# GpSimd's extra piece of an attention step directly behind the masking of the keys, ahead of its wait for the statistics

## The chip, the cores and the metric

The kernel runs on one core of one Trainium2 chip. TensorE (PE) multiplies matrices, VectorE (DVE), ScalarE (ACT) and GpSimd (POOL) work element by element, SyncE (SP) issues DMAs. The metric is the device time of one execution in microseconds. The kernel before takes 1256.31 us (median of 3 runs, 1255.82 to 1256.45).

## What is computed

Two layers on `x` of 128 sequences x 64 positions x 128 features, float32. Cut to what matters:

```python
x = x + xattn0(layernorm(x), ctx, ctx)     # 16 heads of 8, causal softmax attention
x = x + ffn0(layernorm(x))                 # 64 experts, the top 8 by affinity, sigmoid weights
x = x + xattn1(layernorm(x), ctx, ctx)     # autocorrelation attention (rfft, top 6 lags)
x = x + ffn1(x)                            # ternary weights, clipped activations

def xattn0(q, k, v):
    qh, kh, vh = split(q @ Wq + bq), split(k @ Wq + bq), split(v @ Wq + bq)
    scores = einsum('bhqd,bhkd->bhqk', qh, kh) / sqrt(8) * mask - 1e10 * (1 - mask)
    return merge(einsum('bhqk,bhkd->bhqd', softmax(scores), vh)) @ Wo + bo
```

The change lies in the first of these four, the function `attention`. While it runs, other engines' spare time also goes to preparing the second: the experts' weights are split into a high and a low part (the low part is the weight less its rounded high part), and the first chunk's norm and routing (which experts a token takes, with which weights) are computed in its last steps.

## The kernel before

`attention` works on 64 tiles, two sequences of 64 positions on the 128 partitions. It is a pipeline written by hand: each engine has one `step(t, r)`, called for t = 0 to 69, in which it does one stage of several tiles at once, each by its lag behind t. Steps 0 to 15 are written out, steps 16 to 47 are a loop of four steps (r = t mod 4, 8 turns), steps 48 on are written out again. Inside an engine the order is the order of the code; between engines only semaphores order the work.

In a step t the stages that matter here are:

- GpSimd: `expand` of tile t-3 (L405, "masking": the keys are spread over four heads with a mask of heads), which waits for ScalarE's copy of the queries and keys (L543); then, for tile t, variance plus epsilon (L428), which waits for VectorE's aggregate, and the power -1/2 (L430); then the bias added to the residual of tile t-5 (L433); then, in some steps, an extra piece.
- VectorE: reciprocal (L289) and scaling (L294) of tile t-6, which wait for TensorE's weighing; the shift of the scores of tile t-4 (L283); the norm of tile t-1 (L273, one `tensor_scalar` from SBUF to SBUF); the statistics of tile t (L264, L268); the output added to the residual of tile t-6 (L300), which waits for TensorE's output projection (L652); in some steps a piece of routing; the row maximum of tile t-3 (L278), which waits for TensorE's scores.
- TensorE: weighing of the values of tile t-6 (L647), which waits until VectorE's L300 of the tile before has freed the bank; transposes (L608, L615, L626, L630), projections (L637, L638, L652); mask and scores of tile t-3 (L594, L600), which wait for GpSimd's masked keys.
- ScalarE: the high part of the weights (L568, one piece in each looped step), copies out of PSUM, the exponential (L558).

The extra pieces of GpSimd are: in steps 13 and 14 two pieces of the chunk norm (L738, L745); in the loop the low part of the weights (L413), of the up weights in steps with r = 1 and of the down weights in steps with r = 3, 16 in all; in steps 48 to 51 and 57 to 60 the split of the biases (L465 to L496); in steps 52 to 56 the routing's ends (L858 to L861), its two powers (L866), the denominator (L870) and the routing's low part (L841). The norm's roots in step 12 and the routing's weights (step 61) and gates (step 63) are further ones. The code of the low part waits for the high part:

```python
def low_part(t, k):
    cols = bass.ds((t // 4 - peeled // 4) * piece, piece)
    wait_apart(pool, high, t + 2 * k + 2, idle["pool"])
    nc.gpsimd.tensor_tensor(cst[("wul", "wdl")[k]][:, cols], raw[:, k, cols], ...)
```

Of the kernel before, what the change touches and what calls it, by code (L numbers as in the profile page):

```python
# [27 lines left out]
ALU = mybir.AluOpType  # L28
# [20 lines left out]
def at_least(eng, sem, value):  # L49

    if isinstance(value, int) and value <= 0:
        return
    eng.wait_ge(sem, value)


def wait_apart(eng, sem, value, idle):

    at_least(eng, sem, value)
    if not isinstance(value, int):
        eng.sem_inc(idle, 1)  # L60
# [17 lines left out]
def live(t, lag, count):  # L78

    return not isinstance(t, int) or 0 <= t - lag < count  # L80
# [11 lines left out]
def attention(nc, cst, dram, x, ctxT, x_res, raw, held, norms, routing, sem, n_tiles=TILES):  # L92
# [8 lines left out]
    with ExitStack() as mem:  # L101
        def sb(name, shape, dt=F32):
            return mem.enter_context(nc.sbuf_tensor(name, shape, dt))
# [5 lines left out]
        mv = sb("a_mv", [P, 2, 2])  # L109
        ve = sb("a_ve", [P, 2, 1])  # L110
        rstd = sb("a_rstd", [P, 2, 1])
# [38 lines left out]
        stats = sem("a_stats_done")  # L150
        mean_var = sem("a_mean_var")
        rstd_done = sem("a_rstd_done")
        normed = sem("a_normed")
        biased = sem("a_biased")
# [23 lines left out]
        idle = {e: sem(f"a_idle_{e}") for e in ("dve", "sp", "pool")}  # L178
# [34 lines left out]
        with nc.Block() as block:  # L213
# [179 lines left out]
            def _(pool):  # L393
# [8 lines left out]
                def expand(t, k):  # L402
                    at_least(pool, qk_out, t + 1)
                    at_least(pool, scored, t - 1)
                    nc.gpsimd.tensor_tensor(kx[:, k], qkT[:, k, 1].unsqueeze(2).to_broadcast([P, 2, 4, S]),  # L405
                                            cst["hmask"][:].unsqueeze(1).unsqueeze(3).to_broadcast([P, 2, 4, S]),
                                            ALU.mult).then_inc(keys, 1)
# [5 lines that stand above are left out]
                    nc.gpsimd.tensor_tensor(cst[("wul", "wdl")[k]][:, cols], raw[:, k, cols],  # L413
                                            cst[("wuh", "wdh")[k]][:, cols].bitcast(F32), ALU.subtract).then_inc(raw_read, 1)

                def step(t, r):
                    if isinstance(t, int) and t == 0:
                        pool.wait_ge(preset_dve, 1)
                    if isinstance(t, int) and t == 2:
                        pool.wait_ge(second_landed, 16 * len(second))  # L420
                    if isinstance(t, int) and t == 5:
                        pool.wait_ge(bias_out, 1)
                    if live(t, 3, n_tiles):
                        expand(t - 3, (r - 3) % 2)
                    if live(t, 0, n_tiles):
                        at_least(pool, stats, 2 * t + 2)
                        wait_apart(pool, normed, t - 1, idle["pool"])
                        nc.gpsimd.tensor_scalar(ve[:, r % 2, :], mv[:, r % 2, 1:2], 1e-5, None, ALU.add).then_inc(rstd_done, 1)  # L428
                        at_least(pool, rstd_done, 2 * t + 1)
                        nc.gpsimd.tensor_tensor(rstd[:, r % 2, :], ve[:, r % 2, :], cst["mhalf"][:], ALU.pow).then_inc(rstd_done, 1)  # L430
                    if live(t, 5, n_tiles):
                        at_least(pool, normed, t - 4)
                        nc.gpsimd.tensor_tensor(x_res[:, bass.ds(t - 5, 1), :], x_res[:, bass.ds(t - 5, 1), :],  # L433
                                                cst["boe"][:].unsqueeze(1), ALU.add).then_inc(biased, 1)
                    if isinstance(t, int) and t in bias_parts:
                        bias_parts[t]()
                    if isinstance(t, int) and t == 12:
                        norms.roots(pool, cst["mhalf"], 0, idle["pool"])
                    if isinstance(t, int) and t == 13:
                        norms.centre(x_res, 0)  # L440
                    if isinstance(t, int) and t == 14:
                        norms.scale(pool, 0, idle["pool"])
                    if not isinstance(t, int) and r % 2 == 1:
                        low_part(t - r, r // 2)
                    if isinstance(t, int) and t == looped + 4:
                        routing.ends(pool, nc.gpsimd, "pool", 0)
                    if isinstance(t, int) and t == looped + 5:
                        routing.fourth_powers(pool, nc.gpsimd, "pool", 0, (0,))
                    if isinstance(t, int) and t == looped + 6:
                        routing.fourth_powers(pool, nc.gpsimd, "pool", 0, (1,))  # L450
                    if isinstance(t, int) and t == looped + 7:
                        routing.denominator(pool, nc.gpsimd, "pool", 0)
                    if isinstance(t, int) and t == looped + 8:
                        routing.low_part(pool, 0, 0)
                    if isinstance(t, int) and t == looped + 13:
                        routing.weights(pool, nc.gpsimd, "pool", 0)
                    if isinstance(t, int) and t == looped + 15:
                        routing.gates_of(pool, nc.gpsimd, "pool", 0)
# [35 lines left out]
                def bias_low_on():  # L494
# [3 lines left out]
                bias_parts = {looped: bias_high, looped + 1: bias_rest, looped + 2: bias_first, looped + 3: bias_middle,  # L498
                              looped + 9: bias_add, looped + 10: bias_add_on, looped + 11: bias_low, looped + 12: bias_low_on}
                pipeline(pool, n_tiles, peeled, 4, step, looped)  # L500
                routing.await_turned(pool, 0)
                norms.norm(pool, x_res, cst["mhalf"], 1, idle["pool"])
# [1385 lines left out]
```

## Time and profile before

| | |
|---|---|
| median of 3 runs | 1256.31 us |
| profiled execution, its own time | 1256.63 us |
| span of the profile | 1254.8 us |
| PE busy | 1215.7 us (97%) |
| DVE busy | 1058.4 us (84%) |
| ACT busy | 919.5 us (73%) |
| POOL busy | 766.4 us (61%) |
| mean granted clock of TensorE | 0.99 |

Attention takes the first 295 us of the span, the looped steps lie between 66 and 204 us. A busy engine is one that executes an instruction; a timeline row gives the start, the duration, the engine, the line, the operation and the tensors, and in square brackets how long the engine was idle before and what ended the wait. A row of waits gives the waiting engine and line, what it waited for, the total in us, how often and the longest one.

### The profile page before, as it was taken

The page shows a single profiled execution, that of the slowest core. Times are in us where ns is not written, and L with a number is a line of the kernel's source. Part 1 is how long each engine was busy: PE and PEld are TensorE (multiplying, and loading weights), DVE is VectorE, ACT ScalarE, POOL GpSimd, SP SyncE. Part 2 cuts the span into 40 slices and gives each one's busy share as a digit, 9 for nine tenths or more (in the row PEclk, how much of TensorE's full clock was granted, in tenths as well). Part 3 has the DMA queues.
Part 4 walks back from the last instruction along what each step waited for, and adds up shares of the span by engine and source line. Part 5 has one row for each costly group of instructions (what it writes and reads, how often), then busy time and mean ns, then how long its engine had stood idle before and what let it go on. Part 6 is the DMA issues. An engine that isn't in the chain of part 4 may idle for free. (4 is left out here: it accounts for less than half of the span.)

```text
span 1254.8 us, 28473 instructions
## 1 busy us (share of the span) xinstructions
PE 1215.7 (97%) x9899; PEld 999.9 (80%) x9899; DVE 1058.4 (84%) x2053; ACT 919.5 (73%) x1601; POOL 766.4 (61%) x829
## 2 busy tenths in 40 slices
PE   8999999998999999999999999999999999899986
PEld 6877777777888888888888888888888888799976
DVE  6988988996887987987988978978879876689986
ACT  5898898876777777677776777777777767777761
POOL 4666667863665665655755665656656624477773
PEclk9999999998999999999999999999999999999998
DMA  6411111106777677687777677677777786111004
GB/s 142 107 32 31 31 29 31 37 16 151 173 184 178 165 184 180 160 196 174 172 185 179 178 173 178 179 172 173 184 175 169 184 189 152 39 35 31 19 2 134
DMA packets 126174, 159.99 MB, mean 127 GB/s; under 512 B 20840, under 2 KB 59504, under 8 KB 126064
## 3 DMA queue, kind: packets, MB, share of 16 engines
q1 hardware_dynamic: 120976, 156.16, 51.5%
q10 hardware_dynamic: 5088, 2.43, 0.7%
q8 instruction: 61, 1.00, 0.4%
q14 instruction: 49, 0.40, 0.1%
HBM read 152.25 MB, written 6.29 MB: 126 GB/s over the span
## 5 line engine op out<-in xcount | busy, mean ns | idle before, releaser
L1196 ACT ACTIVATE e_pu<-e_pu 128x1024 f32<-128x1024 f32 x256 | 258.7, 1010 | 203.1 <-PE e_pu L1232 202.9
L1133 DVE TENSOR_TENSOR e_m<-e_pu,raw 128x1024 f32<-128x1024 f32 x256 | 310.0, 1211 | 93.8 <-ACT e_pu L1196 93.7
L1053 POOL TENSOR_TENSOR e_ml<-e_m,e_mh 128x1024 fp32r<-128x1024 f32 x80 | 192.5, 2407 | 145.8 <-ACT e_mh L1206 144.4
L1206 ACT CAST e_mh<-e_m 128x1024 fp32r<-128x1024 f32 x256 | 267.3, 1044 | 4.9 <-DVE e_m L1133 4.9
L1138 DVE TENSOR_TENSOR e_ml<-e_m,e_mh 128x1024 fp32r<-128x1024 f32 x176 | 240.9, 1369 | 25.8 <-ACT e_mh L1206 25.8
L1230 PE MATMUL e_pu<-r_xh,wuh 128*128 128x512 f32 x528 | 214.6, 406 | 0.6 <-PEq L213 0.6
L1242 PE MATMUL e_py<-e_mh,wdl 128*128 128x512 f32 x528 | 209.3, 396 | 0.0
L1231 PE MATMUL e_pu<-r_xh,wul 128*128 128x512 f32 x528 | 209.2, 396 | 0.0
L1232 PE MATMUL e_pu<-r_xl,wuh 128*128 128x512 f32 x528 | 209.2, 396 | 0.0
L1241 PE MATMUL e_py<-e_mh,wdh 128*128 128x512 f32 x528 | 208.0, 394 | 0.0
L1245 PE MATMUL e_py<-e_ml,wdh 128*128 128x512 f32 x528 | 167.4, 395 | 0.1
L1232 PEld LDWEIGHTS e_pu<-r_xl,wuh 128*128 128x128 f32 x528 | 99.6, 189 | 24.1
L1242 PEld LDWEIGHTS e_py<-e_mh,wdl 128*128 128x128 f32 x528 | 99.2, 188 | 24.7
L1245 PEld LDWEIGHTS e_py<-e_ml,wdh 128*128 128x128 f32 x528 | 99.1, 188 | 24.5 <-POOL e_ml L1053 0.5
L1241 PEld LDWEIGHTS e_py<-e_mh,wdh 128*128 128x128 f32 x528 | 99.1, 188 | 23.4
L1230 PEld LDWEIGHTS e_pu<-r_xh,wuh 128*128 128x128 f32 x528 | 99.8, 189 | 22.0 <-issue 0.9
L1231 PEld LDWEIGHTS e_pu<-r_xh,wul 128*128 128x128 f32 x528 | 99.8, 189 | 21.3
L647 PEld LDWEIGHTS pob<-vx,pT 128*64 128x64 f32 x2048 | 67.0, 138 | 34.0 <-issue 30.9
L278 DVE TENSOR_REDUCE mx<-ps 128x16 f32<-128x1024 f32 x64 | 78.0, 1219 | 13.0 <-PE ps L600 10.4
L647 PE MATMUL pob<-vx,pT 128*64 128x18 f32 x2048 | 72.4, 212 | 7.9 <-DVE x_res L300 5.0
L283 DVE TENSOR_TENSOR prob<-ps,mx 128x1024 f32<-128x1024 f32 x64 | 77.7, 1214 | 0.3 <-issue 0.2
L558 ACT ACTIVATE prob<-prob 128x1024 f32<-128x1024 f32 x64 | 69.5, 1086 | 1.6 <-DVE prob L283 1.5
(228 smaller groups left out, 2351.9 us busy)
## 6 DMA issues: line engine op xcount, KB each, us to landing
raw<-gates_scratch SPq DMA_DIRECT2D x512, 256.0 KB, 4.2
x_res<-in_x_dram SPq DMA_DIRECT2D x64, 64.0 KB, 1.9
xcT<-in_ctxT_dram SPq DMA_DIRECT2D x64, 64.0 KB, 2.0
held<-in_ctx_dram SPq DMA_DIRECT2D x32, 128.0 KB, 2.1
raw<-in_L_ffn_W_up_dram SPq DMA_DIRECT2D x4, 512.0 KB, 5.2
raw<-in_L_ffn_W_down_dram SPq DMA_DIRECT2D x4, 512.0 KB, 5.9
gates_scratch<-raw SPq DMA_DIRECT2D x16, 128.0 KB, 2.3
out_dram<-t_res SPq DMA_DIRECT2D x8, 256.0 KB, 2.5
```

The source lines that it names most:

```text
L647: ins = nc.tensor.matmul(po[q, 2 * j:2 * j + 2, :], pT[:, r % 2, j, q], vx[:, r % 4, j, b], start=True, stop=True)
L1053: nc.gpsimd.tensor_tensor(flat(ml[k][:]), flat(m[k][:]), flat(mh[k][:]).bitcast(F32), ALU.subtract).then_inc(m_low[1], 1)
L1133: nc.vector.tensor_tensor(flat(m[r % 3][:]), flat(pu[r % 3][:]), flat(gt[i % SPREAD]), ALU.mult).then_inc(gated, 1)
L1138: nc.vector.tensor_tensor(flat(ml[k][:]), flat(m[k][:]), flat(mh[k][:]).bitcast(F32), ALU.subtract).then_inc(m_low[0], 1)
L1196: nc.scalar.activation(flat(pu[k][:]), flat(pu[k][:]), ACT.Silu).then_inc(silued, 1)
L1206: nc.scalar.copy(flat(mh[k][:]), flat(m[k][:])).then_inc(m_high, 1)
L1230: nc.tensor.matmul(pu[k][:, j, :], cst["wuh"][:, w], xh[:, b, :], start=True, stop=False)
L1231: nc.tensor.matmul(pu[k][:, j, :], cst["wul"][:, w], xh[:, b, :], start=False, stop=False)
L1232: ins = nc.tensor.matmul(pu[k][:, j, :], cst["wuh"][:, w], xl[:, b, :], start=False, stop=True)
L1241: nc.tensor.matmul(py[:], cst["wdh"][:, w], mh[k][:, j, :], start=(i == 0 and j == 0), stop=False)
L1242: nc.tensor.matmul(py[:], cst["wdl"][:, w], mh[k][:, j, :], start=False, stop=False)
L1245: ins = nc.tensor.matmul(py[:], cst["wdh"][:, w], ml[k][:, j, :], start=False, stop=(i == FULL))
```

## The change

The extra piece of a step moves. Before, GpSimd's step is masking, L428, L430, L433, extra piece. After, it is masking, extra piece, and then what were L428, L430 and L433, which are lines 446, 448 and 451 in the changed file. The roots of step 12, the routing's weights and the gates stay behind them.

```diff
                     if live(t, 3, n_tiles):
                         expand(t - 3, (r - 3) % 2)
-                    if live(t, 0, n_tiles):
-                        at_least(pool, stats, 2 * t + 2)
-                        wait_apart(pool, normed, t - 1, idle["pool"])
-                        nc.gpsimd.tensor_scalar(ve[:, r % 2, :], mv[:, r % 2, 1:2], 1e-5, None, ALU.add).then_inc(rstd_done, 1)
-                        at_least(pool, rstd_done, 2 * t + 1)
-                        nc.gpsimd.tensor_tensor(rstd[:, r % 2, :], ve[:, r % 2, :], cst["mhalf"][:], ALU.pow).then_inc(rstd_done, 1)
-                    if live(t, 5, n_tiles):
-                        at_least(pool, normed, t - 4)
-                        nc.gpsimd.tensor_tensor(x_res[:, bass.ds(t - 5, 1), :], x_res[:, bass.ds(t - 5, 1), :],
-                                                cst["boe"][:].unsqueeze(1), ALU.add).then_inc(biased, 1)
                     if isinstance(t, int) and t in bias_parts:
                         bias_parts[t]()
-                    if isinstance(t, int) and t == 12:
-                        norms.roots(pool, cst["mhalf"], 0, idle["pool"])
                     if isinstance(t, int) and t == 13:
                         norms.centre(x_res, 0)
...
                     if isinstance(t, int) and t == looped + 8:
                         routing.low_part(pool, 0, 0)
+                    if live(t, 0, n_tiles):
+                        at_least(pool, stats, 2 * t + 2)
...
+                    if live(t, 5, n_tiles):
...
+                    if isinstance(t, int) and t == 12:
+                        norms.roots(pool, cst["mhalf"], 0, idle["pool"])
                     if isinstance(t, int) and t == looped + 13:
                         routing.weights(pool, nc.gpsimd, "pool", 0)
```

GpSimd's instructions in the loop, before, from the masking of the step with r = 1 to that of the step with r = 2 (wul is the low part of the up weights, raw the loaded weights, wuh their high part, kx the masked keys; L53 and ISA rows are register work and waits):

```order
L405 TENSOR_TENSOR kx<-qkT,hmask 128x512
L53 ISA
L428 TENSOR_SCALAR a_ve<-a_mv 128x1
L53 REGISTER_ALU
L430 TENSOR_TENSOR a_rstd<-a_ve,mhalf 128x1
L433 ISA
L433 TENSOR_TENSOR x_res<-x_res,boe 128x128
L53 REGISTER_ALU
L413 ISA
L413 REGISTER_ALU
L413 TENSOR_TENSOR wul<-raw,wuh 128x528
L405 TENSOR_TENSOR kx<-qkT,hmask 128x512
```

The same stretch of GpSimd after the change:

```order
L405 TENSOR_TENSOR kx<-qkT,hmask 128x512
L53 REGISTER_ALU
L413 ISA
L413 REGISTER_ALU
L413 TENSOR_TENSOR wul<-raw,wuh 128x528
L53 ISA
L446 TENSOR_SCALAR a_ve<-a_mv 128x1
L53 REGISTER_ALU
L448 TENSOR_TENSOR a_rstd<-a_ve,mhalf 128x1
L451 ISA
L451 TENSOR_TENSOR x_res<-x_res,boe 128x128
L405 TENSOR_TENSOR kx<-qkT,hmask 128x512
```

The low part stood directly in front of the second masking and stands directly behind the first. The step with r = 3 changes in the same way.

GpSimd in steps 52 and 53 after the change (raw holds the routing's tensors here, eb the experts' biases):

```order
L405 TENSOR_TENSOR kx<-qkT,hmask 128x512
L858 TENSOR_TENSOR raw<-raw,eb 128x256
L860 TENSOR_SCALAR raw<-raw 128x256
L861 TENSOR_SCALAR raw<-raw 128x256
L446 TENSOR_SCALAR a_ve<-a_mv 128x1
L448 TENSOR_TENSOR a_rstd<-a_ve,mhalf 128x1
L451 TENSOR_TENSOR x_res<-x_res,boe 128x128
L405 TENSOR_TENSOR kx<-qkT,hmask 128x512
L866 TENSOR_TENSOR raw<-raw 128x512
```

Before, the three rows of the ends (L858 to L861) stood behind the statistics and the bias of step 52, in front of the second masking. The other engines' orders are the same before and after.

## Rows read from the trace of the kernel before

**Rows 1.** Waits of the looped steps, 69 to 204 us.

```profile
POOL a_ve L428 <- DVE a_mv L268: 45.0, 32, 2.6
PE pob L647 <- DVE x_res L300: 3.5, 17, 0.4
...
DVE mx L278 <- PE ps L600: 1.8, 8, 0.2
```

**Rows 2.** Timeline of GpSimd over one turn of the loop.

```profile
141.32 0.22 POOL L428 TENSOR_SCALAR a_ve<-a_mv 128x1 f32<-128x1 f32 x1 [1.79 <-DVE a_mv L268]
...
142.57 1.32 POOL L413 TENSOR_TENSOR wul<-raw,wuh  x1
143.84 1.04 POOL L405 TENSOR_TENSOR kx<-qkT,hmask 128x512 f32<-128x512 f32 x1
145.72 0.22 POOL L428 TENSOR_SCALAR a_ve<-a_mv 128x1 f32<-128x1 f32 x1 [0.83 <-DVE a_mv L268]
...
146.97 1.04 POOL L405 TENSOR_TENSOR kx<-qkT,hmask 128x512 f32<-128x512 f32 x1
149.84 0.22 POOL L428 TENSOR_SCALAR a_ve<-a_mv 128x1 f32<-128x1 f32 x1 [1.83 <-DVE a_mv L268]
...
154.45 0.22 POOL L428 TENSOR_SCALAR a_ve<-a_mv 128x1 f32<-128x1 f32 x1 [1.05 <-DVE a_mv L268]
...
155.71 1.04 POOL L405 TENSOR_TENSOR kx<-qkT,hmask 128x512 f32<-128x512 f32 x1
158.53 0.22 POOL L428 TENSOR_SCALAR a_ve<-a_mv 128x1 f32<-128x1 f32 x1 [1.79 <-DVE a_mv L268]
```

**Rows 3.** Timeline of one step, PE and DVE alone.

```profile
145.97 1.11 PE L647 MATMUL pob<-vx,pT 128*64 128x18 f32 x32 [0.18 <-DVE x_res L300]
...
147.12 0.26 DVE L289 RECIPROCAL rden<-pob 128x16 f32<-128x16 f32 x1
...
148.75 0.34 DVE L273 TENSOR_SCALAR a_xn<-x_res,a_mv,a_rstd 128x128 f32 x1
...
149.66 0.29 DVE L300 TENSOR_TENSOR x_res<-x_res,pob 128x128 f32 x1
...
150.09 1.34 PE L647 MATMUL pob<-vx,pT 128*64 128x18 f32 x32
```

**Rows 4.** Timeline, the norm L273 in two other steps of the turn.

```profile
144.41 0.56 DVE L273 TENSOR_SCALAR a_xn<-x_res,a_mv,a_rstd 128x128 f32 x1
...
157.44 0.34 DVE L273 TENSOR_SCALAR a_xn<-x_res,a_mv,a_rstd 128x128 f32 x1
```

**Rows 5.** Timeline, ScalarE's high part in the step with r = 1.

```profile
155.73 0.41 ACT L568 CAST wuh<-raw  x1
```

**Rows 6.** Last steps: three timeline rows, then the norm's group, then a wait.

```profile
205.51 0.22 POOL L428 TENSOR_SCALAR a_ve<-a_mv 128x1 f32<-128x1 f32 x1 [0.59 <-DVE a_mv L268]
...
208.42 1.03 POOL L405 TENSOR_TENSOR kx<-qkT,hmask 128x512 f32<-128x512 f32 x1
...
208.71 0.83 DVE L273 TENSOR_SCALAR a_xn<-x_res,a_mv,a_rstd 128x128 f32<-128x128 f32 x1
...
L273 DVE TENSOR_SCALAR a_xn<-x_res,a_mv,a_rstd 128x128 f32<-128x128 f32 x17 | 8.0, 469 | 0.0
...
PE ps L594 <- POOL kx L405: 1.9, 4, 0.5
```

**Rows 7.** Last steps: a wait, then ScalarE's affinities, ends, masking, norm.

```profile
DVE x_res L300 <- PE pob L652: 2.0, 3, 1.1
...
222.90 0.40 ACT L853 ACTIVATE raw<-pj 128x256 f32<-128x256 f32 x1
...
224.85 0.72 POOL L858 TENSOR_TENSOR raw<-raw,eb 128x256 f32<-128x256 f32 x1
...
226.88 1.03 POOL L405 TENSOR_TENSOR kx<-qkT,hmask 128x512 f32<-128x512 f32 x1
...
228.14 0.34 DVE L273 TENSOR_SCALAR a_xn<-x_res,a_mv,a_rstd 128x128 f32<-128x128 f32 x1
```

More of the change, by code:

```diff
@@ L454, in step @@
                         routing.low_part(pool, 0, 0)
+                    if live(t, 0, n_tiles):
+                        at_least(pool, stats, 2 * t + 2)
+                        wait_apart(pool, normed, t - 1, idle["pool"])
+                        nc.gpsimd.tensor_scalar(ve[:, r % 2, :], mv[:, r % 2, 1:2], 1e-5, None, ALU.add).then_inc(rstd_done, 1)
+                        at_least(pool, rstd_done, 2 * t + 1)
+                        nc.gpsimd.tensor_tensor(rstd[:, r % 2, :], ve[:, r % 2, :], cst["mhalf"][:], ALU.pow).then_inc(rstd_done, 1)
+                    if live(t, 5, n_tiles):
+                        at_least(pool, normed, t - 4)
+                        nc.gpsimd.tensor_tensor(x_res[:, bass.ds(t - 5, 1), :], x_res[:, bass.ds(t - 5, 1), :],
+                                                cst["boe"][:].unsqueeze(1), ALU.add).then_inc(biased, 1)
+                    if isinstance(t, int) and t == 12:
+                        norms.roots(pool, cst["mhalf"], 0, idle["pool"])
                     if isinstance(t, int) and t == looped + 13:
```

## The prediction

> **What bounds the kernel now.** I read the waits of the looped part of attention first [rows 1]. GpSimd waits 45.0 us there, always in front of the step's first statistics piece (L428) for VectorE's aggregate (L268), so GpSimd as a whole is not short of time. TensorE waits for VectorE's add of the output (L300) in 17 steps, VectorE for TensorE's scores in 8. The timeline of one step [rows 3] shows why that is the loop: the weighing L647 starts at 145.97; the reciprocal L289 at 147.12; behind it scaling and shift; the norm L273 at 148.75; behind it statistics and aggregate; the add L300 from 149.66 to 149.95; the next weighing at 150.09, 0.14 behind that add. 145.97 to 150.09 is 4.12 us without a gap, by way of L273. The row maximum L278 stands beside the weighing and is off this circle as long as it starts with it. So everything that delays L273 delays the step.
>
> L273 comes in two lengths. At 148.75 and 157.44 it takes 0.34 us; at 144.41 it takes 0.56 [rows 3, 4]. In the last case GpSimd's masking L405 runs from 143.84 to 144.88 [rows 2], and L273 ends at 144.97, 0.09 behind it. At 208.71 it takes 0.83 us, to 209.54, and L405 ran from 208.42 to 209.45: 0.09 again [rows 6]. The norm, both of whose tensors lie in SBUF, waits until the GpSimd instruction in progress has ended, and then needs 0.09 us. What remains of that instruction under 0.25 us costs nothing (0.34 less 0.09). *By the Trainium skill (SBUF — State Buffer, section "Who interferes with whom") VectorE's two-port modes, which a tensor_scalar can enter, and GpSimd take one port pair as an exclusive lock, and the first to start holds it for its whole instruction. By that rule a norm issued inside any GpSimd piece waits for its end, which the two rows above show; were the port shared instead, a piece would cost the norm only a part of that.*
>
> **The change part by part.** Nothing is added or removed. Each piece of GpSimd's steps up to the routing's low part moves from behind L433 to behind L405 of the same step, hence from in front of one masking to behind the masking before it. VectorE, TensorE, ScalarE and SyncE keep their order, and no DMA is moved.
>
> *The loop, 8 turns of four steps.* From L428 to L428 the four steps take 4.40, 4.12, 4.61 and 4.08 us, 17.21 in all [rows 2].
>
> 1. First low part (L413 on wul, at 142.57). Before, it pushed L405 from 142.57 to 143.84 and so into the norm at 144.41, and that step took 4.40. After, L405 runs from 142.57 (its input is out of ScalarE by then) to 143.6 and no piece runs at 144.41. The step falls to 4.12: -0.28.
> 2. Second low part (wdl). After, it stands behind the L405 that starts at 146.97: 1.00 later, 147.97, to 149.28 (1.31 long). The norm of this step is issued at 148.75, so it waits until 149.28 + 0.09 = 149.37 and not 149.09: +0.28. What this part pushed before was a masking that no norm had to wait for; that step (4.61) keeps its length.
> 3. The first low part in its new place: behind the L405 at 155.71, from 156.71 to 158.02. The norm is issued at 157.44 [rows 4] and ends at 158.11, not 157.78: +0.33. In this step the aggregate-to-L428 distance is 0.05 longer, which is where the extra hundredths come from; I take +0.32.
>
> Sum: -0.28 + 0.28 + 0.32 = +0.32 per turn, 8 turns: **+2.6 us**. Behind a delayed norm the statistics, the add L300 and the weighing all shift; GpSimd's next L428 still finds it idle (158.02 against 158.53 before the shift). The low part's own input, the high part by ScalarE at 155.73, 0.41 us long [rows 5], is there 0.6 us before the piece wants it at 156.71, and in the step with r = 3 likewise, so the new place adds no wait.
>
> *The last 16 steps.* A piece of length E now runs behind L405, 2.25 us after its L428, and lengthens the norm by about E - 1.17 (the norm comes some 3.2 us after L428 there). Before, E plus the masking of 1.04 did the same one step later, by the same amount: 205.51 to 208.42 is 1.25 + 1.66, and 1.66 - 1.17 = 0.49 is what L273 at 208.71 has above 0.34 [rows 6]. All 17 norms from 204 on take 8.0 us [rows 6], 17 x 0.34 = 5.8, so 2.2 us of blocking, of which 0.46 belongs to the routing weights, which stay where they are. Remaining: 1.8. After, by the same subtraction for the other pieces: the bias's high part (E 1.66) 0.49, and 0.13 more because it follows a looped step, whose L428 stands later; the bias's rest (1.13) none; the routing's first power 0.31 (below); its low part (1.27) 0.10; two later pieces of the bias (1.57 each) 0.40 and 0.40, the two of 1.1 none. The two middle pieces of the bias's split and the routing's ends fall into the steps in which L300 waits 2.0 us for TensorE's projection anyway [rows 7], and cost nothing. Together 1.8. TensorE's wait for keys, 1.9 us in 4 steps [rows 6], goes; but in the same steps the blocked norm held the circle up by as much, so I give it nothing (0.2 at most, where the maximum started late). Net: **0.0**, between -0.8 (the high part has two instructions with a gap; if the norm gets in between, its 0.6 goes) and +0.5.
>
> *One wait is added.* The routing's ends (L858) now stand in front of L428 and want the affinities that ScalarE writes at 222.90 + 0.40 = 223.30 [rows 7]. They take 2.03 us (224.85 to 226.88), so to 225.4, and L428, today 1.25 before L858 and so at 223.6, comes 1.8 late. Queued behind it are the root, the bias add and the next masking. The root is wanted by the norm at 228.14 [rows 7] and is done 0.9 behind L428, near 226.3; the masking comes at 225.4 + 1.25 = 226.7, where it is today (226.88). The wait costs nothing; if the margin were used up, up to 1.8 us. Behind that masking stands the first power, 227.7 to 228.7, over the norm issued at 228.14: it ends at 228.79, not 228.48, the 0.31 above.
>
> *The chunk norm's two pieces in steps 13 and 14.* Each is one pass over 512 columns, as the masking is (1.04 us). By the same working the second one blocks a norm by about 0.25. The first starts just as the masking ends on which a norm is already waiting: if GpSimd keeps its turn, a further 1.0. No row shows such a pair for this norm. I take **+0.25**, between 0 and +1.3.
>
> Sum: 2.6 + 0.0 + 0.25 = +2.8 us. The stages behind attention start when it ends, and nothing there moves, so it passes through. Against the profiled execution's own 1256.63 us that is 1259.4; the median of the runs shown, 1256.31, lies 0.3 lower, so **1259.1 us**.
>
> **The rivals.**
>
> - *Hidden behind TensorE, no change.* The step with the first low part's new place has a maximum that waits 0.2 us for the scores (8 such waits, [rows 1]); if that wait took up the delay, and only the rest counted, step 3 of the loop would cost 0.10 and the turn +0.10: +0.8 + 0.25 = 1257.3. Against it: the weighing starts 0.14 behind the add [rows 3] and takes as long as the maximum, so the delay goes by TensorE and not by the maximum.
> - *Faster: the early keys decide.* The place is the norm's port. If the norm is not held by the low part in its new place, the blocks of today go (8 x 0.28, and 1.8 in the last steps) and none comes: -4.0, 1252.3. It decides once the norm starts before the low part does. For it: TensorE's 4 waits for keys. Against: the low part starts at 147.97, the norm at 148.75, 0.78 too late, and the low part reads two tensors just as the masking does. *The Trainium skill's page named above says that the order of issue decides which of the two engines blocks; by that it is the norm here.*
> - *Slower still: GpSimd keeps its turn through two pieces, or the ends' wait reaches the norm.* +1.0 in step 13 and up to 1.8 at the ends: 1260.1 to 1261.9, taken at 1261. For it: consecutive records of GpSimd overlap by 0.05 us (142.57 + 1.32 against 143.84, [rows 2]), so there may be no gap for VectorE. Against: 1.8 us between the late root and its norm.
>
> **How the numbers follow.** Forecast 0.58, hidden 0.19, faster 0.08, slower still 0.15. The forecast's own range is 1258.0 to 1260.1. The range 1256.8 to 1261.1 leaves out the faster case and parts of the outer two. A measurement here tells about 0.2%, 2.5 us, from no change, so the line lies at 1258.8, just under the forecast: some 0.37 of the forecast's chance is above it, and with the slower rival that makes 0.51; 0.21 of it and the hidden case make 0.40; faster 0.09.
>
> **What would show it.** L273 should take 0.34 us where it now takes 0.56, and 0.60 to 0.67 in two of each four looped steps, always ending 0.09 behind L413. From L428 to L428 the turn should read 4.12, 4.40, 4.61, 4.40. The aggregate's wait on GpSimd should fall in the steps with a low part, and TensorE's wait for L405 should be gone. L858 should start at ScalarE's affinities and L428 behind it late, with no norm waiting for L430. I am wrong if L273 stays at 0.34 with L413 beside it, or if L647 starts no later than now behind a long L273.

## The result and the profile after

| | before | after |
|---|---|---|
| median, 15 runs each | 1256.31 us | 1258.12 us |
| lowest to highest | 1254.10 to 1257.33 | 1257.22 to 1260.04 |
| after / before | | 1.0022, 95% interval 1.0015 to 1.0030 |
| profiled execution, its own time | 1256.63 us | 1259.83 us |
| span | 1254.8 us | 1258.0 us |
| mean granted clock of TensorE | 0.99 | 0.992 |

The changed kernel is slower by 0.22%, which is +2.8 us (1.9 to 3.8) of 1256. The forecast was 1259.1, a rise of 2.8; the two medians lie 1.8 apart, and the interval of the ratio holds both. In the changed file L428, L430 and L433 are L446, L448 and L451; the other lines named here kept their numbers.

The first view after is that of the waits in the looped steps, 69 to 204 us (total us, times, longest):

```profile
POOL a_ve L446 <- DVE a_mv L268: 45.8, 31, 2.6
PE pob L647 <- DVE x_res L300: 7.8, 23, 0.4
...
DVE mx L278 <- PE ps L600: 1.7, 8, 0.2
```

Against [rows 1], GpSimd waits as long as before (45.8 against 45.0 us) and VectorE too (1.7 against 1.8). What grew is TensorE's wait for the add L300, from 3.5 to 7.8 us and from 17 to 23 times: in the circle that the prediction named, VectorE is late and TensorE waits for it. No wait of GpSimd or VectorE shows the loss, since the norm's delay stands in its duration. The timeline of GpSimd over one turn shows the moved pieces (a turn is one pass of the loop's four steps):

```profile
143.38 0.22 POOL L446 TENSOR_SCALAR a_ve<-a_mv 128x1 f32<-128x1 f32 x1 [0.83 <-DVE a_mv L268]
...
147.51 0.22 POOL L446 TENSOR_SCALAR a_ve<-a_mv 128x1 f32<-128x1 f32 x1 [1.83 <-DVE a_mv L268]
...
149.76 1.32 POOL L413 TENSOR_TENSOR wdl<-raw,wdh  x1
151.91 0.22 POOL L446 TENSOR_SCALAR a_ve<-a_mv 128x1 f32<-128x1 f32 x1 [0.83 <-DVE a_mv L268]
...
156.51 0.22 POOL L446 TENSOR_SCALAR a_ve<-a_mv 128x1 f32<-128x1 f32 x1 [2.30 <-DVE a_mv L268]
...
158.76 1.31 POOL L413 TENSOR_TENSOR wul<-raw,wuh  x1
160.90 0.22 POOL L446 TENSOR_SCALAR a_ve<-a_mv 128x1 f32<-128x1 f32 x1 [0.83 <-DVE a_mv L268]
```

GpSimd's wait for the statistics fell in the two steps with a low part (0.83 each, where they had 1.79 and 1.83) and rose in the other two (1.83 and 2.30, where they had 0.83 and 1.05) [rows 2], so its sum stayed.

The norms of the same turn, and the add behind one of them, from VectorE's timeline:

```profile
146.42 0.34 DVE L273 TENSOR_SCALAR a_xn<-x_res,a_mv,a_rstd 128x128 f32 x1
...
150.59 0.57 DVE L273 TENSOR_SCALAR a_xn<-x_res,a_mv,a_rstd 128x128 f32 x1
...
151.73 0.29 DVE L300 TENSOR_TENSOR x_res<-x_res,pob 128x128 f32 x1
...
159.50 0.65 DVE L273 TENSOR_SCALAR a_xn<-x_res,a_mv,a_rstd 128x128 f32 x1
```

And TensorE's weighing behind that add:

```profile
152.16 1.32 PE L647 MATMUL pob<-vx,pT 128*64 128x18 f32 x32 [0.41 <-DVE x_res L300]
```

The piece on wdl ends at 149.76 + 1.32 = 151.08 and the norm at 150.59 + 0.57 = 151.16; the piece on wul ends at 160.07 and the norm at 160.15. Both norms end 0.08 behind GpSimd: they are held, which below always means that a norm issued while a piece runs ends just behind it and not after its own 0.34 us. The norm that took 0.56 beside a pushed masking [rows 4] takes 0.34, at 146.42. The weighing starts at 152.16, 0.14 behind the add's end at 152.02, as in [rows 3].

For the stages of attention I use the start of the row maximum L278 as the mark, in the first looped step (step 16, 68.78 in both traces), in step 47 and in step 64, the last that has a norm. VectorE's timeline of before:

```profile
201.62 1.23 DVE L278 TENSOR_REDUCE mx<-ps 128x16 f32<-128x1024 f32 x1
...
275.48 1.23 DVE L278 TENSOR_REDUCE mx<-ps 128x16 f32<-128x1024 f32 x1 [0.48 <-PE ps L600]
```

The same of after:

```profile
68.78 1.22 DVE L278 TENSOR_REDUCE mx<-ps 128x16 f32<-128x1024 f32 x1
...
204.48 1.22 DVE L278 TENSOR_REDUCE mx<-ps 128x16 f32<-128x1024 f32 x1
...
277.50 1.23 DVE L278 TENSOR_REDUCE mx<-ps 128x16 f32<-128x1024 f32 x1 [0.49 <-PE ps L600]
```

| stage, by these marks | before | after | difference |
|---|---|---|---|
| loop (first looped step to step 47) | 132.84 | 135.70 | +2.86 |
| last steps (step 47 to step 64) | 73.86 | 73.02 | -0.84 |

The loop loses what was forecast and a little more; the last steps give 0.84 back. The two traces' spans differ by 3.2 us and these marks by 2.0; the experts' first matrix product is 1.58 later. The rest, 1.6 us, arises behind attention, where both kernels issue the same work. From that product to the end the profiled execution takes 959.3 us before and 960.9 after; in the twelve experiments below, which leave this stretch alone, it takes 958.8 to 961.0. A difference of 1.6 there lies inside what one execution differs from another, and nothing shows that it belongs to the change.

### The profile page after: what moved, and what is told of

The parts are those of the page before. It is cut to its first block and busy times, and to the rows that moved or that the text cites. A ratio compares the mean times of both kernels' runs of the same rounds, so it can differ in the third digit from the quotient of the medians.

```text
span 1258.0 us, 28473 instructions
## 1 busy us (share of the span) xinstructions
PE 1216.5 (97%) x9899; PEld 1000.1 (79%) x9899; DVE 1059.4 (84%) x2053; ACT 920.5 (73%) x1601; POOL 767.5 (61%) x829
## 5 line engine op out<-in xcount | busy, mean ns | idle before, releaser
L278 DVE TENSOR_REDUCE mx<-ps 128x16 f32<-128x1024 f32 x64 | 77.8, 1216 | 11.7 <-PE ps L600 11.0
L858 POOL TENSOR_TENSOR raw<-raw,eb 128x256 f32<-128x256 f32 x16 | 19.3, 1204 | 85.7 <-ACT raw L853 85.7
```

## The experiments

Each kernel was run beside the kernel before on one chip. "Loop" and "last steps" are measured by the marks above, and stand against 132.84 and 73.86. Kernels with the same loop repeat its length within 0.24 us (132.84 and 132.92; 135.70 and 135.68; with halves 131.31, 131.55 and 131.54). Experiments 3, 4 and 7 to 11 have one execution each and are read for the durations in its trace.

**1. Only the low parts of the loop moved** (e1_loop_only). The other extra pieces stay where they were.

```diff
                         expand(t - 3, (r - 3) % 2)
+                    if not isinstance(t, int) and r % 2 == 1:
+                        low_part(t - r, r // 2)
...
-                    if not isinstance(t, int) and r % 2 == 1:
-                        low_part(t - r, r // 2)
```

> Of the kernel before, only the low parts of the loop (L413 in the old numbering) are moved directly behind the masking; all other pieces stand where they stood. Theory (a piece that runs when the norm is issued holds the norm until 0.09 us behind its end): the turn of four steps takes 17.53 us and not 17.21, the norm 0.66 and 0.57 us in the steps with a low part; TensorE's first matmul of the experts starts 2.6 to 2.9 us later than before (295.5), the time is 2.6 to 2.9 us above before's. Rival (the early masking decides and the blocks are a wash): turn at or under 17.2 us, time as before.

Measured: 1258.81 us (1257.68 to 1260.38), ratio 1.0025 (1.0015 to 1.0035). Loop 135.68, which is +2.84; last steps 73.85, unchanged. The whole loss of the loop belongs to this one edit. The experts' first matrix product is at 297.32, 1.80 and not 2.6 to 2.9 later than before: in this trace the first looped step already stands 0.89 earlier (67.89), which the marks leave out.

**2. Everything but the low parts moved** (e2_rest_only). The changed kernel with the low part back behind the bias, by the same two lines.

> All pieces but the low parts of the loop are moved; the low parts stay behind the bias. Theory after the trace of the changed kernel: the last 16 steps lose about 0.8 us, the chunk norm's second piece costs 0.2: first matmul of the experts 0.6 us earlier than in the kernel before, time 0.6 lower, hard to tell from no change. The prediction as it stood (last steps 0.0, chunk norm +0.25): 0.25 later. Rival (ends' wait for the affinities costs the path its 1.9 us): 1 us or more later.

Measured: 1255.54 us (1253.85 to 1257.26), ratio 1.0000 (0.9992 to 1.0009). Loop 132.92, unchanged; last steps 72.96, which is -0.90. So the gain in the last steps belongs to the pieces outside the loop. The experts' first product is 0.63 earlier (294.89), as the reading of the trace after the change had it and not as the prediction did (0.25 later); in the time, 0.6 us can't be told from none. The two halves add up: +2.84 - 0.90 = +1.94, where the whole change has 2.86 - 0.84 = 2.02.

**3. A norm over 127 of 128 columns** (e3_norm_127). Can the norm's form decide whether GpSimd holds it? The last column is left out, and the tile is filled with zeros once at the start.

```diff
-                    nc.vector.tensor_scalar(xn[:, r % 2, :], x_res[:, bass.ds(t, 1), :], mv[:, r % 2, 0:1],
+                    nc.vector.tensor_scalar(xn[:, r % 2, 0:127], x_res[:, bass.ds(t, 1), 0:127], mv[:, r % 2, 0:1],
...
+                nc.vector.memset(xn[:], 0.0)
```

> The changed kernel, but the norm writes and reads 127 of the 128 columns (column 127 of the normalised tile stays zero: that part of the computation is left out). [...] Lock theory: the norm takes about 0.41 us (0.07 more than 0.34) in every step, with or without a GpSimd piece beside it, none over 0.45; the turn takes 3 x 4.19 + 4.63 = 17.2 us and not 17.53; the first matmul of the experts is at 294 to 296 us and not 297.1. Rival (the norm waits for GpSimd for another reason, a semaphore or the memory): still 0.57 to 0.67 beside L413.

Norms of one turn, VectorE's timeline:

```profile
137.69 0.64 DVE L273 TENSOR_SCALAR a_xn<-x_res,a_mv,a_rstd 128x127 f32 x1
...
146.29 0.57 DVE L273 TENSOR_SCALAR a_xn<-x_res,a_mv,a_rstd 128x127 f32 x1
```

Neither a longer norm nor a freed one: 0.64 and 0.57 beside the low part, and 0.34 in the step between them. The expectation fell on both numbers. The turn takes 17.38 us, between the two expected values of 17.2 and 17.53: from maximum to maximum the step with r = 1 is 0.11 shorter (4.18 instead of 4.29). Experiment 9 has the same 17.38 and 4.18; why is open. The one run took 1254.05 us.

**4. Another kind of piece in the same place** (e4_dtype). The low parts are left out (they stay zero); pieces that read one tensor, 1.57 us long where the low part takes 1.31, take their place, from bf16 at r = 1 and from float32 at r = 3. ScalarE's wait for the low parts goes too, here and in experiments 7 and 8.

```diff
-                    if not isinstance(t, int) and r % 2 == 1:
-                        low_part(t - r, r // 2)
+                    if not isinstance(t, int) and r == 1:
+                        nc.gpsimd.tensor_scalar(scr_out[0:3], scr16[0:3], cst["mhalf"][0:3], None, ALU.mult)
+                    if not isinstance(t, int) and r == 3:
+                        nc.gpsimd.tensor_scalar(scr_out[0:3], scr32[0:3], cst["mhalf"][0:3], None, ALU.mult)
```

> The changed kernel, but in the looped steps the low parts are replaced (the low halves of the weights are left out and stay zero): in steps with r = 1 by a GpSimd tensor_scalar over 3 partitions x 512 from bf16 to bf16, in steps with r = 3 by the same from float32 to bf16. Both should take about 1.57 us and be running when the norm is issued. Theory A (any piece holds the norm): norm 0.9 us in both. Theory B (as two bf16 pieces in the changed kernel's last steps suggest): 0.34 us in the steps with r = 1 and 0.8 to 0.95 us in those with r = 3.

Timeline of GpSimd and VectorE at both pieces:

```profile
145.85 1.57 POOL L439 TENSOR_SCALAR a_scr_out<-a_scr,mhalf 3x512 bf16<-3x512 bf16 x1
146.56 0.34 DVE L276 TENSOR_SCALAR a_xn<-x_res,a_mv,a_rstd 128x128 f32 x1
...
154.11 1.57 POOL L441 TENSOR_SCALAR a_scr_out<-a_scr,mhalf 3x512 bf16<-3x512 f32 x1
154.86 0.34 DVE L276 TENSOR_SCALAR a_xn<-x_res,a_mv,a_rstd 128x128 f32 x1
```

Both norms take 0.34 and end with 0.52 and 0.48 us of the piece still to run. Neither data type holds the norm, so neither theory had it right. What both pieces share against the low part is that they read one tensor, and that they cover 3 partitions and not 128. (The time, 1261.69, carries the zero fills at the start and is not compared.)

**5. The low part in halves** (e5_halves). The kernel before, each low part cut in two pieces of 264 columns, one in each of the four looped steps, behind the masking. The wait of ScalarE for raw_read counts twice as many.

```diff
+                def low_half(t, k):
+                    cols = bass.ds((t // 4 - peeled // 4) * piece + (k % 2) * (piece // 2), piece // 2)
+                    wait_apart(pool, high, t + k + 1, idle["pool"])
+                    nc.gpsimd.tensor_tensor(cst[("wul", "wdl")[k // 2]][:, cols], raw[:, k // 2, cols],
+                                            cst[("wuh", "wdh")[k // 2]][:, cols].bitcast(F32), ALU.subtract).then_inc(raw_read, 1)
...
                         expand(t - 3, (r - 3) % 2)
+                    if not isinstance(t, int):
+                        low_half(t - r, r)
```

> The kernel before, but the low part of the weights is done in halves, one behind the masking of every looped step (264 columns, about 0.66 us each, the half whose high part ScalarE has just made). Theory: the piece ends 2.25 + 0.66 = 2.9 us behind the variance piece, the norm reads some 3.3 behind it, so no norm in the loop is held: 0.34 us everywhere, the turn 3 x 4.12 to 4.19 plus 4.56 = 16.9 to 17.1 us against 17.21 before, first matmul of the experts 1.5 to 2.6 us earlier than with the whole parts behind the bias, time 1.5 to 2.6 lower than before's. Rival (the early place itself costs, by the register work or the wait in front of the statistics): turn 17.5 as in the changed kernel.

Timeline of one looped step, GpSimd and the norm:

```profile
149.76 0.75 POOL L420 TENSOR_TENSOR wul<-raw,wuh  x1
150.93 0.34 DVE L273 TENSOR_SCALAR a_xn<-x_res,a_mv,a_rstd 128x128 f32 x1
```

Measured: 1254.49 us (1253.26 to 1256.90), ratio 0.9987 (0.9977 to 0.9996). The piece ends at 150.51, 0.42 before the norm is issued; over the loop the norms average 336 ns. Loop 131.31, which is -1.53; last steps 73.49. The same work, in the same place of a step but spread over all four steps, in pieces that end before the norm comes: faster than before. In one step of each turn it is close: the piece ends at 138.11 and the norm is issued at 138.09, and takes 0.34. A half takes 0.75, more than half of 1.31.

**6. Halves, and only those of the other pieces that gain** (e6_best). Halves in the loop; the bias's pieces and the later routing pieces in the new place; chunk norm, ends and first power in the old.

```diff
-                    if isinstance(t, int) and t == 13:
-                        norms.centre(x_res, 0)
-                    if isinstance(t, int) and t == 14:
-                        norms.scale(pool, 0, idle["pool"])
...
-                    if isinstance(t, int) and t == looped + 4:
-                        routing.ends(pool, nc.gpsimd, "pool", 0)
-                    if isinstance(t, int) and t == looped + 5:
-                        routing.fourth_powers(pool, nc.gpsimd, "pool", 0, (0,))
```

(on the changed kernel with halves; the eight lines return behind the bias of the step)

> Halves in the loop as in e5, the chunk norm's pieces, the routing's ends and first power in their old place, the bias pieces and the other routing pieces in the new one. Theory: the loop's gain of e5 (1.5 to 2.6 us) plus the last steps' (0.8 from the changed kernel and another 0.4 because the ends no longer wait for the affinities in front of the statistics): 2.7 to 3.8 us below before. Rival (the last steps' gain was luck of phase and turns over when the loop ends elsewhere): no better than e5.

Timeline in the last steps:

```profile
228.75 1.04 POOL L873 TENSOR_TENSOR raw<-raw 128x512 f32<-128x512 f32 x1
228.78 1.09 DVE L273 TENSOR_SCALAR a_xn<-x_res,a_mv,a_rstd 128x128 f32<-128x128 f32 x1
```

Measured: 1253.78 us (1252.61 to 1256.14), ratio 0.9982 (0.9973 to 0.9990), the fastest kernel of the study by its ratio, though its interval overlaps that of experiment 5. Loop 131.55, last steps 73.10. By the ratio it gains 2.3 and not 2.7 to 3.8: with the first power moved back, the second one, directly behind the masking, begins 0.03 before the norm and holds it for its whole length, 1.09; that step is 0.74 longer than before.

**7. A long piece of one tensor, and one that only writes** (e7_kinds). The low parts are left out again.

```diff
+                    if not isinstance(t, int) and r == 1:
+                        nc.gpsimd.tensor_scalar(scr[:, 0:1024], scr[:, 0:1024], 1.0, None, ALU.mult)
+                    if not isinstance(t, int) and r == 3:
+                        nc.gpsimd.memset(scr[:].bitcast(BF16)[:, 0:1600], 1.0)
```

> The changed kernel, but in the looped steps the low parts are replaced (the weights' low halves are left out and stay zero): with r = 1 by a GpSimd tensor_scalar with one tensor over 128 partitions x 1024 float32, with r = 3 by a memset of 128 x 1600 bf16, which reads nothing. Each should take about 1.5 us and be running when the norm is issued. Theory C (only pieces that read two tensors hold the norm, since e4's pieces with one tensor did not): 0.34 us in both. Theory D (e4's pieces let it through because they cover 3 partitions): norm 0.8 to 0.9 with r = 1. Lock on the write side: 0.8 to 0.9 with r = 3 too.

Timeline of GpSimd and VectorE at the two pieces:

```profile
111.82 2.80 POOL L436 TENSOR_SCALAR a_scr<-a_scr 128x1024 f32<-128x1024 f32 x1
112.44 0.52 DVE L274 TENSOR_SCALAR a_xn<-x_res,a_mv,a_rstd 128x128 f32 x1
...
120.06 1.43 POOL L438 MEMSET a_scr<- 128x1600 bf16 x1
120.91 0.65 DVE L274 TENSOR_SCALAR a_xn<-x_res,a_mv,a_rstd 128x128 f32 x1
```

The fill, which reads nothing, holds the norm to its own end (121.49, norm to 121.56). The piece of one tensor holds it too, but only to 112.96, 1.14 behind its own start and 1.66 before its end. So reading a second tensor is not what holds a norm, and covering 128 partitions is not enough to hold it to the end; this one-tensor piece, 2.80 us where 1.5 was expected, lets go before it ends.

**8. The same one-tensor piece at two distances from the norm** (e8_phase). The low parts are left out.

```diff
+                    if not isinstance(t, int) and r in (0, 3):
+                        nc.gpsimd.tensor_scalar(scr_out[0:3], scr[0:3], cst["mhalf"][0:3], None, ALU.mult)
```

> The changed kernel with the loop's low parts left out and in their place, with r = 3 and r = 0, a GpSimd tensor_scalar over 3 partitions x 640 from float32 to bf16, about 1.95 us long. The norm asks about 1.0 us into the piece with r = 3 and about 1.45 us into it with r = 0. Theory E (a piece of this kind lets the norm through in its first 1.1 us and holds it afterwards, as the one such piece did that held the norm in the changed kernel, L492): norm 0.34 with r = 3 and 0.6 to 0.8 with r = 0. Theory C (a piece with one tensor never holds it): 0.34 in both.

Timeline of GpSimd and VectorE at the step with r = 0 and at that with r = 3:

```profile
123.73 1.89 POOL L437 TENSOR_SCALAR a_scr_out<-a_scr,mhalf 3x640 bf16<-3x640 f32 x1
124.89 0.82 DVE L275 TENSOR_SCALAR a_xn<-x_res,a_mv,a_rstd 128x128 f32 x1
...
136.87 1.89 POOL L437 TENSOR_SCALAR a_scr_out<-a_scr,mhalf 3x640 bf16<-3x640 f32 x1
137.62 0.34 DVE L275 TENSOR_SCALAR a_xn<-x_res,a_mv,a_rstd 128x128 f32 x1
```

Issued 0.75 into the piece the norm takes 0.34; issued 1.16 into it, it is held to 0.09 behind the end. One instruction, two answers: it depends on when the norm comes.

**9. The norm as three groups of 42 columns** (e9_norm_3x42). Two columns are left out. The line is cut here; the tile is filled with zeros once at the start.

```diff
+ nc.vector.tensor_scalar(xn[:, r % 2, 0:126].rearrange("p (g c) -> p g c", c=42), x_res[:, bass.ds(t, 1), 0:126].rearrange(...), mv[:, r % 2, 0:1],
```

> The changed kernel, but the norm covers 126 of 128 columns as 3 groups of 42 (the last two columns of the normalised tile stay zero: that part is left out), so that its outer dimension is odd on both sides; e3's 127 columns in one row had left the norm as it was. If the form decides (two ports only for an even outer dimension): norm near 0.41 us, never held, turn near 17.2 us. If the form does not decide: 0.34, and 0.65 and 0.57 beside L413, turn 17.5, as in e3. I think the second likelier after e3.

VectorE's timeline, the norm beside the low part wul:

```profile
140.00 0.65 DVE L273 TENSOR_SCALAR a_xn<-x_res,a_mv,a_rstd 128x126 f32 x1
```

Held like the 128-column one (beside the wdl of the same turn it takes 0.57). The form of the norm, in the shapes tried, does not decide. The turn takes 17.38, as in experiment 3, and not 17.5.

**10 and 11. Only one of the two low parts moved** (e10_only_r3, e11_only_r1): experiment 1 with `r == 3`, and with `r == 1`, the other one staying behind the bias.

> The kernel before with the down weights' low part (r = 3) alone moved behind the masking; the up weights' (r = 1) stays behind the bias. By the working of the forecast the whole cost is this one's: its norm 0.57 in place of 0.34, nothing comes back, turn 17.21 + 0.28 = 17.5 us; the r = 2 step keeps its 0.56 norm. Rival (the two only cost together): 17.2.

> The kernel before with the up weights' low part (r = 1) alone moved. Its norm 0.66 in place of 0.34 (+0.32), the norm one step later 0.34 in place of 0.56 (-0.28): turn 17.21 + 0.04 = 17.25 us. Rival: 17.5 (the late norm costs and the early masking gives nothing back).

From the low parts' rows (ns lowest/median/highest, first to last start), with wdl alone moved:

```profile
L413 POOL TENSOR_TENSOR wul<-raw,wuh x8: 1302/1312/1319, 72.8 to 195.0; - x8
```

With wul alone moved:

```profile
L413 POOL TENSOR_TENSOR wul<-raw,wuh x8: 1302/1307/1310, 70.2 to 191.3; - x8
```

Seven turns lie between first and last: 17.46 and 17.30 us a turn. By the same row before has 17.14 and after 17.53. Moving wdl costs 0.32, moving wul 0.16, together 0.48 where both have 0.39. The prediction had +0.28 for wdl, and -0.28 and +0.32, so +0.04, for wul. That wdl is the dearer one holds; wul costs more than it said, and the two don't add up exactly. The freed norm is there (0.34 in the step with r = 2), so the excess stands elsewhere: from maximum to maximum the step with r = 0 takes 4.53 to 4.55 in experiment 11, and 4.33 to 4.49 before. Why is open. Beside the moved wdl the norm takes 0.61 and not 0.57, since here it is issued 0.05 earlier in the piece. The one run of each gave 1258.02 and 1256.21 us.

**12. Halves, with every routing piece back in the old place** (e12_best2): experiment 6, with the second power, denominator and low part of routing moved back too.

```diff
-                    if isinstance(t, int) and t == looped + 6:
-                        routing.fourth_powers(pool, nc.gpsimd, "pool", 0, (1,))
-                    if isinstance(t, int) and t == looped + 7:
-                        routing.denominator(pool, nc.gpsimd, "pool", 0)
-                    if isinstance(t, int) and t == looped + 8:
-                        routing.low_part(pool, 0, 0)
```

> As e6, but all routing pieces of steps 52 to 56 in their old place, since e6's second power behind a masking that itself stood behind the first power held one norm for 1.09 us. The bias pieces stay in the new place, the chunk norm's in the old, the low part in halves. Theory: last steps 0.6 to 0.7 us shorter than e6's, time 2.7 to 3.2 us below before (ratio about 0.9977). Rival: the phase of the bias pieces moves and one of them holds a norm: no better than e6.

Timeline of GpSimd and VectorE in the last steps:

```profile
245.49 1.15 POOL L495 TENSOR_TENSOR bias<-bias,s_bpart 3x512 bf16<-3x512 bf16 x1
245.55 1.18 DVE L273 TENSOR_SCALAR a_xn<-x_res,a_mv,a_rstd 128x128 f32<-128x128 f32 x1
...
249.51 1.68 POOL L499 TENSOR_SCALAR s_bpart<-held,ident 3x512 bf16<-3x512 f32 x1
250.41 0.34 DVE L273 TENSOR_SCALAR a_xn<-x_res,a_mv,a_rstd 128x128 f32<-128x128 f32 x1
```

Measured: 1254.70 us (1252.47 to 1256.69), ratio 0.9990 (0.9981 to 0.9999); last steps 73.06 against 73.10 in experiment 6. The powers no longer hold a norm, but a bias piece now starts directly behind a late masking (244.50 to 245.54) and 0.06 before a norm, and holds it for 1.18: the rival of the expectation. The low bias piece L499, which is L492 in the changed kernel and held a norm there, lets it through here, at the same distance of 0.90. The intervals of 6 and 12 overlap; 12 is no gain over 6.

## Why the prediction held, point by point

*The circle.* Right. L413 beside L273 makes the norm 0.57 and 0.65 (forecast were 0.60 to 0.67; beside wdl the norm is issued 0.05 later than I worked with and ends where forecast, 0.08 behind the piece), and the four distances from L446 to L446 read 4.13, 4.40, 4.60 and 4.39 where 4.12, 4.40, 4.61 and 4.40 were forecast. The waits show it at TensorE, not at GpSimd. Experiment 1 gives the loop's loss to the low parts alone; 5 takes the loss away by making the piece end before the norm.

*The loop's size.* +2.86 against +2.6. The turn before takes 17.14 on average over seven turns, the turn from which I worked 17.21; after has 17.53, as forecast from that turn (17.53). So the working started from a turn 0.07 longer than the average, which hid 0.07 of the loss in each turn; that the turn after came out to the hundredth is partly luck. The norms confirm the size: over the loop they average 480 ns, and 395 before.

```profile
L273 DVE TENSOR_SCALAR a_xn<-x_res,a_mv,a_rstd 128x128 f32 x31 | 14.9, 480 | 0.0
```

In this group of VectorE (columns: count, busy us, mean ns) 31 norms, 70 to 204 us of after, take 14.9 us; the same window of before has 12.3. The difference, 2.6, is the blocking itself. The other 0.26 I can't place to an instruction; from maximum to maximum, in before the step with r = 0 varies between 4.34 and 4.49, and in after it is 4.70.

*The chunk norm.* Right: from the maximum of step 13 to that of step 15 it takes 8.19 where it took 7.97, +0.22 against +0.25. GpSimd did not keep its turn against a norm that was already waiting: the norm ran from 54.82 for 0.47, to 0.09 behind the masking, although the next piece's record begins at 55.16.

*The added wait.* Right: in the timeline of GpSimd and VectorE below, L858 starts once ScalarE has written the affinities (225.33 + 0.40), L446 comes behind it at 227.95, and no norm waits for a root.

```profile
225.81 0.73 POOL L858 TENSOR_TENSOR raw<-raw,eb 128x256 f32<-128x256 f32 x1 [1.89 <-ACT raw L853]
...
227.95 0.21 POOL L446 TENSOR_SCALAR a_ve<-a_mv 128x1 f32<-128x1 f32 x1
...
230.20 1.04 POOL L866 TENSOR_TENSOR raw<-raw 128x512 f32<-128x512 f32 x1
230.56 0.76 DVE L273 TENSOR_SCALAR a_xn<-x_res,a_mv,a_rstd 128x128 f32<-128x128 f32 x1
```

The first power, in the last two rows, held a norm for 0.76 where 0.65 was forecast.

*The last 16 steps, the mis-sized term.* "Net: 0.0"; measured: -0.84. The forecast had norms held for 0.49 + 0.13 by the bias's high part, 0.31 and 0.10 by the routing's power and low part, and 0.40 and 0.40 by two later pieces of the bias, 1.83 in all. By the norms' rows after, counted above 0.34, it is 0 for the high part, 0.42, 0.13, 0 and 0.42, and 0.03 for the bias's rest: 1.00. Two steps of the working failed. The high part was taken as one piece of 1.66 us that lasts until the norm; it is two instructions, and the norm came when the first had 0.23 left and went through, close to the case that the prediction had named for its lower bound. And not every piece holds a norm to its end. The timeline of after, GpSimd and VectorE, in these steps:

```profile
206.85 0.88 POOL L465 TENSOR_SCALAR held<-held 3x256 f32<-3x256 f32 x1
207.50 0.34 DVE L273 TENSOR_SCALAR a_xn<-x_res,a_mv,a_rstd 128x128 f32<-128x128 f32 x1
...
214.75 1.60 POOL L474 TENSOR_SCALAR bias<-s_bpart,ident 3x512 bf16<-3x512 bf16 x1
215.56 0.34 DVE L273 TENSOR_SCALAR a_xn<-x_res,a_mv,a_rstd 128x128 f32<-128x128 f32 x1
...
246.38 1.63 POOL L484 TENSOR_SCALAR s_bpart<-s_bpart,ident 3x512 bf16<-3x512 bf16 x1
247.21 0.34 DVE L273 TENSOR_SCALAR a_xn<-x_res,a_mv,a_rstd 128x128 f32<-128x128 f32 x1
...
254.34 1.57 POOL L492 TENSOR_SCALAR s_bpart<-held,ident 3x512 bf16<-3x512 f32 x1
255.24 0.76 DVE L273 TENSOR_SCALAR a_xn<-x_res,a_mv,a_rstd 128x128 f32<-128x128 f32 x1
```

The high part's second instruction starts at 207.79 only. Below it, two one-tensor pieces with 0.8 us left let the norm through in 0.34; one held it for 0.76, to 0.09 behind its end. That last one is near an edge: issued 0.89 to 0.90 into this same piece, the norm took 0.34 in experiments 4, 9 and 12 and 0.76 or 0.77 in after and experiments 2, 3, 6, 7 and 8, and where it took 0.34 in experiment 9 that step is 0.25 shorter, so a part of this stage's time hangs on a hundredth. Experiments 4, 7 and 8 isolate the behaviour. *The Trainium skill (SBUF — State Buffer, section "Who interferes with whom") lets the engine that issued first keep the port pair for the whole of its instruction. The rows agree for the low part (0.07 to 0.09 behind it, every time) and disagree for these two pieces, so here the measurement decides.*

A middle piece of the bias (L480) held a norm for 0.27 as well, but its step is no longer than before: there L300 waits for TensorE anyway, as forecast. From the norms alone the -0.84 does not follow, though. All 17 take 7.5 us and not 8.0 [rows 6]; but in experiment 1, where only the loop was touched, they take 7.7, and its last steps are as long as before. TensorE's wait for L405 fell from 1.9 us [rows 6] to 0.5; the forecast had it gone and gave it nothing. The three waits that go stand in steps 49, 58 and 60, which shrink by 0.57, 0.44 and 0.51 where their norms shrink by 0.46, 0.41 and 0.43, so they can be worth some 0.2 there. How the rest divides is open.

*The sum.* By the marks: 2.86 + 0.22 - 0.84 = 2.2 of attention, against 2.8 forecast. The experts begin only 1.58 later in the profiled pair: 0.44 less than the mark of step 64 (2.02), a stretch of 20 us in which nothing was moved. The medians differ by 1.8, and the ratio's interval, 1.9 to 3.8, holds the 2.2. That the ratio's 2.8 equals the forecast to the tenth is luck: the loop came out 0.3 dearer and the last steps 0.8 cheaper, and the medians and the marks both say less. **Open:** 1.6 us of the profiled pair behind attention, which the spread of that stretch covers (958.8 to 961.0). The 15 times of after lie in two groups (eleven from 1257.2 to 1258.8, four from 1259.8 to 1260.0), and the profiled one is of the upper.

*The rivals.* "Hidden": no, the weighing shifted by the whole delay, and the maximum's wait did not shrink. "Faster": the norm was held in the loop; its mechanism, a norm that is not held, is real in the last steps alone. "Slower still": neither cause appeared. A norm that already waits goes through at the seam of two pieces (54.82). Experiments 6 and 12 show something near it, for 1.09 and 1.18 us, but there the norm comes 0.03 and 0.06 behind the start of the second piece and is held by that one alone.

## What to carry to other kernels

When a small VectorE instruction on the critical circle changes its duration, look at what GpSimd is executing at that moment: the wait hides in the duration and stands among no waits of either engine. Place GpSimd's filler so that it ends before that instruction is issued, and cut it if it does not fit; here 16 pieces of 1.31 us directly behind the masking made the loop 2.8 us longer than in their old place, and 32 pieces of 0.75 us directly behind the masking made it 1.5 shorter. And look at the seams: a norm that comes just behind the start of a second piece (0.03 and 0.06 here) is held for all of it.

## What the runs showed of the hardware that was not expected

- With GpSimd `tensor_tensor` (1.03 to 1.33 us long) and with a fill (1.43 us), every norm issued more than 0.28 us before the end was held to 0.07 to 0.10 behind it: 202 norms in the fourteen traces, without an exception. With 0.25 us or less left, the norm took its 0.34, save the one of experiment 6 at the start of the next piece.
- A GpSimd `tensor_scalar` over one tensor does not hold VectorE's norm for its whole length. Norms issued 0.53 to 0.84 us into such pieces of 1.57 to 1.90 us took 0.34; issued 0.89 to 0.90 in, three took 0.34 and six 0.76 or 0.77; issued 1.15 or more in, all were held to the end. A piece of 1.57 that lets a norm through at 0.90 takes 1.68. In the piece of 2.80 us a norm issued 0.62 in went through at 1.14. Why a one-tensor piece lets go is open.
- In experiment 2 a norm issued 0.40 into such a piece took 0.36, so an opening that starts only some way into the piece is not the whole of it (its timeline, GpSimd and VectorE):

```profile
212.73 1.57 POOL L474 TENSOR_SCALAR bias<-s_bpart,ident 3x512 bf16<-3x512 bf16 x1
213.13 0.36 DVE L273 TENSOR_SCALAR a_xn<-x_res,a_mv,a_rstd 128x128 f32<-128x128 f32 x1
```

- A norm over 127 columns, or 3 groups of 42, is as short (0.34) and as much held as one over 128.
- Half of a low part (264 of 528 columns) takes 0.75 us and not 0.66.
